# Weight halves reordered, counts read without a stride, and four unread products on TensorE in a fused attention and mixture-of-experts kernel

## The reference

```python
xn = _layernorm(x, axis=-1)
x = x + attn(xn, ...) + ffn(xn, ...)

# attn: an RWKV time mix
k, v = xn @ key_w.T, xn @ value_w.T
r = sigmoid(xn @ recep_w.T)
wkv = _wkv_scan(time_decay, time_first, k, v)
attn = (r * wkv) @ out_w.T

# ffn: 8 experts, the best 2 of each token, and one shared expert
logits = xt @ gate_w.T + gate_b
scores = softmax(logits)
top_w, top_i = top_k(scores, 2)
gate_dense = sum(one_hot(top_i, E) * top_w[..., None], axis=1)
h = silu(xt @ w1e.T + b1e) * (xt @ w3e.T + b3e)      # per expert, 256 wide
outs = h @ w2e.T + b2e
y = einsum('etd,te->td', outs, gate_dense)
z = silu(xt @ ws1.T + bs1) * (xt @ ws3.T + bs3) @ ws2.T + bs2
```

## Time and profile before

| what | us |
|---|---|
| median of 3 runs | 474.6 (473.55 to 476.1) |
| the profiled execution | 473.8 |
| its span | 472.0 |
| first expert product starts | 71.06 |
| TensorE busy | 440.8 |
| VectorE busy | 365.9 |
| ScalarE busy | 241.6 |
| POOL busy | 230.3 |

### The profile page before, as it was taken

How to read it: one execution, slowest core, us unless ns; L and a number is a source line. 1 busy time by engine, 2 the same in 40 slices (tenths; PEclk the granted TensorE clock), 3 DMA queues, 4 the chain that set the end, 5 groups by cost and what they waited for, 6 DMA issues and landing times.

```text
span 472.0 us, 8323 instructions
## 1 busy us (share of the span) xinstructions
PE 440.8 (93%) x2534; PEld 370.8 (79%) x2534; DVE 365.9 (78%) x684; ACT 241.6 (51%) x396; POOL 230.3 (49%) x224
## 2 busy tenths in 40 slices
PE   0998687979999999999999899999999999999997
PEld 0562455858888888888888778798888989898987
DVE  5976968968787887878766689995968787877863
ACT  4777734678668595966765532333324132324131
POOL 3333747434858666488854377651433415160000
PEclk9999679999999999999999999999999999999999
DMA  7999923245764865443473773826153443431001
GB/s 228 341 305 395 228 69 101 80 178 190 253 215 146 264 184 167 135 134 117 123 208 109 288 273 97 274 63 214 56 165 115 126 152 123 156 113 67 24 24 44
DMA packets 45858, 77.24 MB, mean 164 GB/s; under 512 B 5908, under 2 KB 32252, under 8 KB 45820
## 3 DMA queue, kind: packets, MB, share of 16 engines
q1 hardware_dynamic: 37580, 55.87, 34.1%
q0 software_dynamic: 8240, 20.88, 17.0%
HBM read 48.52 MB, written 28.21 MB: 163 GB/s over the span
## 4 chain that ended last, share of the span: by engine, by line
PE 64%; DVE 14%; POOL 9%; issue 7%; ACT 4%; DMA 1%; SPq 0%; DVEq 0%; POOLq 0%; ACTq 0%
PE ps_g L1109 11%; PE ps_y L1109 6%; PE ps_w L1569 5%; PE ps_w L1571 5%; PE ps_w L1570 5%; PE ps_w L1635 5%; PE ps_w L1636 5%; PE ps_w L1634 5%; POOL xg L1032 4%; PE ps_G L619 3%; PE ps_x L1103 2%; PE ps_h L1129 2%; PE ps_T L605 2%; PE ps_v L1570 1%; PE ps_r L1571 1%
## 5 line engine op out<-in xcount | busy, mean ns | idle before, releaser
L1032 POOL DMA_INDIRECT xg<-xn_rows,tile_tok x71 | 71.4, 1005 | 26.7 <-issue 18.6
L1545 POOL DMA_INDIRECT yg<-expert_rows,rows x64 | 67.9, 1061 | 23.6 <-issue 17.1
L1109 PE MATMUL ps_g<-w_hi,x_hi 128*128 x142 | 56.2, 396 | 2.2 <-DVE x_lo L1264 2.2
L1109 PE MATMUL ps_g<-w_lo,x_hi 128*128 x142 | 56.3, 396 | 0.0
L1109 PE MATMUL ps_g<-w_hi,x_lo 128*128 x142 | 56.1, 395 | 0.0
L1676 ACT ACTIVATE sact<-ps_w,vec_b 128x512 f32<-128x512 f32 x32 | 22.0, 687 | 58.4 <-PE ps_w L1571 58.4
L1569 PE MATMUL ps_w<-col_hi,s_hi 128*128 128x512 f32 x128 | 50.5, 395 | 0.4 <-DVE shid L1787 0.4
L1570 PE MATMUL ps_w<-col_lo,s_hi 128*128 128x512 f32 x128 | 50.2, 392 | 0.0
L1571 PE MATMUL ps_w<-col_hi,s_lo 128*128 128x512 f32 x128 | 50.2, 392 | 0.0
L1109 PE MATMUL ps_y<-w_hi,h_hi 128*128 x142 | 43.2, 304 | 1.3 <-DVE h_lo L1280 1.3
L1273 DVE TENSOR_TENSOR hid<-ps_g,act 128x512 f32<-128x512 f32 (+1 forms) x36 | 23.7, 659 | 24.4 <-ACT act L1185 24.4
(11 more groups left out here) (255 smaller groups left out, 1276.9 us busy)
## 6 DMA issues: line engine op xcount, KB each, us to landing
expert_rows<-y SPq DMA_DIRECT2D x35, 256.0 KB, 2.2
w_lo<-w_all SPq DMA_DIRECT2D x16, 384.0 KB, 9.9
table<-mix_tables SPq DMA_DIRECT2D x8, 768.0 KB, 6.2
xn_rows<-xn SPq DMA_DIRECT2D x16, 256.0 KB, 8.1
xn_columns<-xT SPq DMA_DIRECT2D x8, 512.0 KB
col<-xn_columns SPq DMA_DIRECT2D x8, 512.0 KB, 5.0
res<-x SPq DMA_DIRECT2D x16, 256.0 KB, 2.9
out<-res SPq DMA_DIRECT2D x16, 256.0 KB, 2.2
```

The costliest lines, as they stand in the source:

```text
L1032: pool.indirect_dma_start(out=xg[b][:, t, :], out_offset=None, in_=xn_d[:, :], in_offset=bass.IndirectOffsetOnAxis(ap=tile_tok[:, first_ti ...
L1109: mm = nc.tensor.matmul(out, x[:, k, :], w[:, ds(e, 1), k, cols].rearrange("p o n -> p (o n)"), start=(k == 0 and n == 0), stop=(last and ...
L1545: pool.indirect_dma_start(out=yg[a.buf(2)][:, k, q, :], out_offset=None, in_=y_d[:, :], in_offset=bass.IndirectOffsetOnAxis(ap=picked[a.bu ...
```

## The change

- TensorE: three float32 products of the identity with itself, 512 columns wide, into `ps_G[1]` ahead of the first turn, and one behind it. The bank is overwritten later and nobody reads them.
- The counts: the product now reads `hot` in the order in which it lies, and writes into `ps_cnt` with a stride of 32 numbers.
- `ntile` counts slots, not tiles: adding and subtracting 128 * 2^23 in float32 rounds to whole tiles. Two operations take the place of three, `last_b` is scaled by 1/128, and the last operation on `place` is a plain add.
- ScalarE: `made_hi` 0 to 3 and `made_lo` 0 to 3 stand ahead of the exponentials. `HIGH` is 16: all of `split_hi` is in this stage, ahead of `terms`, and the rest of them in the next stage is gone.
- TensorE: `rest` 0 to 3 ahead of the one-hot products, `rest` 4 and 5 behind them.
- VectorE: `LOW` is 8: `split_lo` 0 to 3 ahead of the difference of `terms`, 4 to 7 behind it, 8 and 9 behind `x_lo` of group 0, 10 and 11 behind `x_lo` of group 1.
- TensorE loads the expert numbers of groups 0 and 1 ahead of the first `turn_x`.

```diff
-        MADE, BOTH, HIGH, LOW = 4, 6, 13, 2
+        MADE, BOTH, HIGH, LOW = 4, 6, 16, 8
...
+        WHOLE = float(P << 23)
...
-            for i in range(2):
+            for i in range(MADE):
                 made_hi(act, i)
+            for i in range(MADE):
+                made_lo(act, i)
             nc.scalar.activation(early[:, 0:1], gb[:], ACT.Exp)
...
-            for i in range(2, MADE):
-                made_hi(act, i)
-            for i in range(2):
-                made_lo(act, i)
             act.wait_ge(s_xn, NSTEP)
             act.wait_ge(s_xna, NSTEP)
             for i in range(MADE, HIGH):
                 split(i)
-            for i in range(2, MADE):
-                made_lo(act, i)
...
+            def busy():
+                nc.tensor.matmul(ps_G[1][:].rearrange("p (q n) -> p q n", q=Q), ident[:],
+                                 ident[:, None, :].broadcast_to([P, Q, P]), start=True, stop=True)
+
             pe.wait_ge(s_const, 7)
+            for i in range(3):
+                busy()
             for i in range(NSTEP + 2):
                 if i < NSTEP:
                     turn(At(0, i, NSTEP))
+                if i == 0:
+                    busy()
...
-                    mm = nc.tensor.matmul(ps_cnt[:, h, :].rearrange("p (e j) -> p e j", e=E), sums[:],
-                                          hot[:, k].rearrange("p j e -> p e j"), start=(k == 0), stop=(k == TOPK - 1))
+                    mm = nc.tensor.matmul(ps_cnt[:, h, :].rearrange("p (e j) -> p j e", e=E), sums[:], hot[:, k],
+                                          start=(k == 0), stop=(k == TOPK - 1))
...
-            for i in range(FIRST):
+            for i in range(MADE):
                 rest(pe, i)
...
-            for i in range(FIRST, BOTH):
+            for i in range(MADE, BOTH):
                 rest(pe, i)
...
-            own.link(nc.vector.tensor_scalar(ntile_i[:], filled[:, :, NT - 1], float(P - 1), float(P), ALU.add,
-                                             ALU.max))
-            own.link(nc.vector.tensor_scalar(ntile_i[:], ntile_i[:], 7, None, ALU.arith_shift_right))
-            own.link(nc.vector.tensor_copy(ntile[:], ntile_i[:]))
+            own.link(nc.vector.tensor_scalar(ntile[:], filled[:, :, NT - 1], (P - 1) / 2, WHOLE, ALU.add, ALU.add))
+            own.link(nc.vector.tensor_scalar(ntile[:], ntile[:], WHOLE, float(P), ALU.subtract, ALU.max))
             own.link(nc.vector.tensor_tensor_scan(out=last[:], data0=ones_f[:, 0:E], data1=ntile[:],
                                                   initial=0.0, op0=ALU.mult, op1=ALU.add))
-            nc.vector.tensor_copy(last_b[:], last[:])
             own.link(nc.vector.tensor_tensor(start[:], last[:], ntile[:], ALU.subtract))
-            own.link(nc.vector.scalar_tensor_tensor(out=place, in0=start[:, None, :].broadcast_to([P, NT, E]),
-                                                    scalar=float(P), in1=place, op0=ALU.mult, op1=ALU.add))
+            nc.vector.tensor_scalar(last_b[:], last[:], 1.0 / P, None, ALU.mult)
+            own.link(nc.vector.tensor_tensor(place, place, start[:, None, :].broadcast_to([P, NT, E]), ALU.add))
...
+            for i in range(4):
+                split_lo(dve, i)
             dve.wait_ge(s_terms, 4)
             nc.vector.tensor_tensor(terms[:, :, E:2 * E], dense[:], terms[:, :, 0:E], ALU.subtract
                                     ).then_inc(s_terms, 1)
-            for i in range(LOW):
+            for i in range(4, LOW):
                 split_lo(dve, i)
...
-            es = {}
             pe.wait_ge(s_tok, 1)
+            es = {a: experts(a) for a in range(2)}
             turn_x(0)
...
-            for i in range(HIGH, E * KC):
-                split_hi(act, i)
             cut_x(2)
...
-            for i in range(LOW, 5):
-                split_lo(dve, i)
             cut_x(0)
-            for i in range(5, 8):
+            for i in range(8, 10):
                 split_lo(dve, i)
             hidden(0)
             cut_x(1)
-            for i in range(8, 12):
+            for i in range(10, 12):
                 split_lo(dve, i)
             cut_x(2)
```

More of the change, by code:

```diff
@@ L806, in vector @@
                                                   data0=keep[:].rearrange("p e j -> p (e j)"),
-                                                  data1=ps_cnt[:, 1, :], initial=0.0,
-                                                  op0=ALU.mult, op1=ALU.add))
+                                                  data1=ps_cnt[:, 1, :], initial=0.0, op0=ALU.mult, op1=ALU.add))
             own.link(nc.vector.tensor_tensor(place.rearrange("p j e -> p e j"), filled[:], prefix, ALU.add))
-            own.link(nc.vector.tensor_scalar(ntile_i[:], filled[:, :, NT - 1], float(P - 1), float(P), ALU.add,
-                                             ALU.max))
-            own.link(nc.vector.tensor_scalar(ntile_i[:], ntile_i[:], 7, None, ALU.arith_shift_right))
-            own.link(nc.vector.tensor_copy(ntile[:], ntile_i[:]))
+            own.link(nc.vector.tensor_scalar(ntile[:], filled[:, :, NT - 1], (P - 1) / 2, WHOLE, ALU.add, ALU.add))
+            own.link(nc.vector.tensor_scalar(ntile[:], ntile[:], WHOLE, float(P), ALU.subtract, ALU.max))
             own.link(nc.vector.tensor_tensor_scan(out=last[:], data0=ones_f[:, 0:E], data1=ntile[:],
                                                   initial=0.0, op0=ALU.mult, op1=ALU.add))
-            nc.vector.tensor_copy(last_b[:], last[:])
             own.link(nc.vector.tensor_tensor(start[:], last[:], ntile[:], ALU.subtract))
-            own.link(nc.vector.scalar_tensor_tensor(out=place, in0=start[:, None, :].broadcast_to([P, NT, E]),
-                                                    scalar=float(P), in1=place, op0=ALU.mult, op1=ALU.add))
+            nc.vector.tensor_scalar(last_b[:], last[:], 1.0 / P, None, ALU.mult)
+            own.link(nc.vector.tensor_tensor(place, place, start[:, None, :].broadcast_to([P, NT, E]), ALU.add))
             own.link(nc.vector.tensor_tensor(prod[:], hot[:], place[:, None].broadcast_to([P, TOPK, NT, E]),
@@ L1151, in tensor @@
                     mm.then_inc(c_turn, 1)
-            es[0] = experts(0)
             up(0, es[0])
             turn_x(1)
-            es[1] = experts(1)
             up(1, es[1])
@@ L1347, in vector @@
             dve.wait_ge(t_carry, 1)
[L1348 to L1349 removed]
+            assert LOW == 8
             cut_x(0)
[L1351 removed]
+            for i in range(8, 10):
                 split_lo(dve, i)
```

1 line of the change is left out of this document (removed).

## The result

| what | before | after |
|---|---|---|
| median of 22 runs each, us | 474.55 (472.49 to 477.1) | 476.99 (474.42 to 479.98) |
| profiled execution | 473.8 | 476.54 |
| its span | 472.0 | 474.7 |
| mean granted clock of TensorE in it | 0.985 | 0.968 |
| first expert product starts | 71.06 | 70.26 |

The ratio after to before is 1.0037, with a 95% interval of 1.0021 to 1.0054: 0.4% slower, surely slower than before, though inside the half per cent that was called no change. The forecast was 472.0 and its range ended at 474.8, so the median lies 2.2 us above the range.

A forecast was written before the change was run, and what follows sets the result against it. TensorE, 93% busy, bounds the kernel, so only time ahead of the first expert product counts. Earlier steps' 1.8 us mostly hide behind the landing at 62.2; 2.6 us sooner gives 472.0 as median, range 470.3 to 474.8.

The forecast's parts named there:

- Products of the identity: Around TensorE's first turns: second turn and gate 2.1 us sooner, about 0.6 us surviving; range 0.6 gained to 0.6 lost.
- Unstrided counts: Four count products at L663: reading in order saves 1.0 us; bounds 1.3 us gained to 1.8 us lost.
- The rival that rested on a slow strided write: Strided writes slow the counts by up to 1.8 us and the clock doesn't rise sooner; 473.6 us, chance 0.22.
- VectorE's chain: Behind the counts: three small operations become two, saving about 0.2 us; reordering `last_b` and `start` gives 0 within 0.1.
- The weight halves: Ahead of the experts: two rests, not four, behind the one-hot products; `x_lo` and first expert product 2.6 us sooner.
- the wait ahead of split 14: On ScalarE ahead of `terms`: it stands at split 14 by about 61, waiting for expert 7's last accumulate at 62.2.
- it follows the loads in the saturated queues, not the compute, so it doesn't move: POOL's last accumulate, ahead of split 14: issued at 56.51, it lands 5.7 us later, at 62.2.
- the first rival: Last accumulate lands sooner or VectorE's 1.4 us `tile_exp` stall is missed: about 3.5 us gained, 471.1 us; chance 0.15.
- The slow rival: TensorE enters the experts at the lower clock; first two groups and x transposes take 5.1 us more: 477.1; chance 0.08.
- Nothing after it: Loop behind the first expert products: same work in the same order, so the distance at 110 us equals that at 68.5.

The follow-up runs named there:

- e2_counts: Kernel before with only the counts changed to read `hot` unstrided; 473.62 us, ratio 0.9978 to the kernel before.
- e12_no_order: Kernel after with the weight halves and the load of expert numbers back in the old order; 472.71 us, ratio 0.9933 to the kernel before.
- e5_wait: Kernel after plus three unread identity products in TensorE's gaps, and VectorE waiting for POOL ahead of its seventh one-hot batch; 473.61 us, ratio 0.9966 to before.
- e1_products: Kernel before with only the four products of the identity added; 474.07 us, ratio 0.9982 to the kernel before.
- e3_order: Kernel before with only the new order of the weight halves and the earlier load of expert numbers; 476.41 us, ratio 1.0028 to the kernel before.
- e9_order_fill: Kernel before with the new order of the weight halves plus three unread identity products in TensorE's later gaps; 476.47 us, ratio 1.0022 to before.
- e10_before_fill: Kernel before with three unread identity products behind the last rest and ahead of the first two expert groups; 476.52 us, ratio 1.0021.

## Why the prediction was wrong

The order of the causes is the prediction's own.

**Products of the identity: right.** The first gates take 1.88 us in the timeline and not 2.96 (2.75 on the chain of the earlier trace rows). But the turns aren't at 0.87 from the start: in the kernel after the clock falls at 11.2 and is up again at 14.7, and the first two turns take 1.57 and 1.41 us. (In the kernel before the windows there give a granted clock of 1.00 although the first turns take 1.94 us; the prediction took its lower level from the durations alone.) What survives to the last logits, as ScalarE reads them, is 0.77 us (35.95 against 36.72), for 0.6 forecast.

**Unstrided counts: right.** From their start to VectorE's scan 1.13 us instead of 2.06: 0.93 for 1.0 forecast. Both `e2_counts` and the kernel after show it:

```profile
40.91 0.60 PE L667 MATMUL ps_T<-hot,before 128*128 128x256 bf16 x2 [0.80 <-DVE hot L787]
41.31 0.64 PE L667 MATMUL ps_T<-hot,ones 128*128 128x256 bf16 x2
...
41.98 0.69 DVE L809 TENSOR_TENSOR_SCAN map<-keep,ps_T 128x256 f32<-128x256 f32 x1 [1.13 <-PE ps_T L667]
```

A product every 0.20 us, with its output written at a stride of 32 numbers. The rival that rested on a slow strided write didn't happen. The Trainium skill (SBUF — State Buffer, Door 1, its box on cachelines) says that non-contiguous access in PSUM slows matmuls significantly; this measurement contradicts it for such writes. Its other half, the penalty for reads from SBUF across 16-byte lines, agrees (0.44 us for the strided read of the same 256 columns). What the prediction doesn't have at all is what else went with the strided read: in some executions of the kernel before the clock falls at it, and in none of the twelve of `e2_counts`.

**VectorE's chain: the direction right, the size half.** `prod` starts at 44.77 instead of 46.84. From the scan (L809, before L805) to it are 2.79 us instead of 3.17, so this edit gives 0.38 for 0.2 forecast. The other 0.2 is the exchange of `last_b` and `start`, which was priced at 0 within 0.1.

**The weight halves: the order came out, two prices didn't.** The rests fit ahead of the one-hot products (they end at 49.1, as forecast), these end at 60.4 (forecast 61.1) and the wait ahead of split 14 is there. The step "it follows the loads in the saturated queues, not the compute, so it doesn't move" failed: the accumulate was issued at 56.52, as forecast, and landed at 64.03 instead of 62.2. Its time on POOL is not its own but depends on what VectorE does beside it, and by running earlier VectorE had its unbroken batches there (its last reduction or cast ahead of 59.49 is the cast at 55.42). The stall of VectorE on `tile_exp` was missed, as the first rival hoped (0.25 us for 1.79), but the landing came later, not sooner. That the issue was on time isn't a given either: it was at 58.67 in `e2_counts` and 61.26 in `e12_no_order`. "POOL waits for the loads before each accumulate" misreads, which gives "issue" and no load for the last one. Everything behind it kept the forecast distances (copies, `terms`, 2.5 us of splits, the constants), so the first product was at 70.26, 1.8 later than 68.45. Of the 2.6 us forecast 0.8 were left.

**The clock: the step that failed.** The slow rival was described with its place, its price and its point ("It decides if the clock isn't up by the end of the second rest"), and it happened: at 64.95 the granted clock stood at 0.50, and its 477.1 us stand beside 476.99 measured. It got a chance of 0.08 through one sentence: "at the lower level those two rests alone are nearly 4 us of unbroken work, and in the old trace it rose 2.5 us after the rests began." That the two rests would be nearly 4 us of work was right (60.42 to 64.95, 4.5 us), and the clock didn't rise in them. The 2.5 us (2.8 by the 0.74 of its window: 62.76 to 65.5) were read off one rise as if they were a distance that the chip keeps. `e12_no_order` shows that they aren't: there the clock rose 5.7 us after the rests began. The row of before said only that the clock had come back 2.8 us into four rests in a row, and the change took two of the four away. The price was nearly right by luck: 1.26 + 0.42 + 1.74 = 3.4 us were lost where 5.1 were priced (the clock rose within the second group), but only 0.8 was gained where 2.6 was forecast.

**Nothing after it** was missed: the distance at 83 us is the same as at the end.

## What to carry to other kernels

Work on an engine that no longer sets the end may still be what keeps its clock up. Before wide products are moved off the path ahead of the busiest stretch of TensorE, read from the windows at which clock that stretch would start and, where the clock rose once in the old trace, count it as one event and not as a rule (here the same distance came out at 2.5 to 5.7 us). Compare the granted clock of the profiled execution with that of the others, too: the kernel before had two kinds. Where TensorE has to wait there anyway, products that nobody reads are a cheap trial: three of them turned 0.4% slower into 0.3% faster. Once the wait is gone they stand on the chain themselves. And the duration of a POOL transfer is only good as long as the same work of VectorE stands beside it.

## What the runs showed of the hardware

- **VectorE against POOL's indirect transfers.** An accumulate (L394) takes 1.54 us where VectorE stands still. Among the float16 operations that make the one-hot matrices some take 1.54 to 2.51 us and others 3.75 to 6.84, and the long ones end 1.4 to 1.5 us after VectorE begins a reduction or stops. It goes both ways: a cast of 71 numbers on VectorE took 1.79 us beside the clearing of `terms` on POOL in the kernel before and 0.25 in the kernel after, and `tile_tok` (L865) took 1.09 instead of 0.20 and ended at 62.0 as the clearing of `terms` on POOL did (60.40 + 1.54 = 61.94). The Trainium skill (SBUF — State Buffer, section "SBUF: two separate sides") says that VectorE and GpSimd share a pair of ports that one of them holds for a whole instruction, that GpSimd can't write the descriptors of its transfers while VectorE has it in a two-port mode, and that an operation of VectorE with two inputs in SBUF holds it only against an operation of GpSimd that reads SBUF. `e5_wait` agrees that the transfer waits for VectorE, 3.79 against 1.54, and the operations that it waits for here have two inputs. Why some transfers among them don't wait neither the page nor a run tells.
- **A strided read can cost twice.** The four products of 256 strided columns took 1.98 us instead of 1.05, and in some executions the granted clock fell under them or right behind them, at 42.5 to 43.9 us. It did so in the profiles of `e1_products`, `e3_order`, `e9_order_fill` and `e10_before_fill`, four of the five profiles with the strided read (the kernel before is the fifth), and in none of the nine without it. The twelve executions of `e2_counts` all had a mean granted clock of 0.986.
- **The granted clock fell while TensorE ran the one-hot products in every profile**, between 51 and 60 us, and came back only behind them. No experiment aimed at that fall.
